# Binning: the spreading copies move from ScalarE to GpSimd, and four lane columns from VectorE to ScalarE

## The reference, cut to what matters

```
x = layernorm(x + L0(x, w, a, src, dst))       # exp(leaky_relu([x[src], x[dst]] @ w) @ a), normalised per src, summed per dst
x = layernorm(x + L1(x, W, A_left, A_right))   # four heads, normalised per src, summed per src
```

## Time and profile before

| | us |
|---|---|
| median of 3 runs | 3259.68 (3258.47 to 3259.81) |
| span of the profiled execution | 3274.5 |
| PE busy | 3060.7 (93%) |
| DVE busy | 3045.9 (93%) |
| ACT busy | 2750.1 (84%) |
| POOL busy | 155.0 (5%) |

### The profile page before, as it was taken

The page is one execution under the profiler, slowest core; times in us unless marked ns, Lnnn a source line. Parts: engine busy times, 40 slices in busy tenths (PEclk is TensorE's granted clock), DMA queues, the critical chain, the costliest instruction groups (busy, mean ns, idle before and its releaser), DMA issues. The chain is left out here.

```text
span 3274.5 us, 101508 instructions
## 1 busy us (share of the span) xinstructions
PE 3060.7 (93%) x40072; PEld 2792.8 (85%) x40072; DVE 3045.9 (93%) x4921; ACT 2750.1 (84%) x6946; POOL 155.0 (5%) x249
## 2 busy tenths in 40 slices
PE   5777699999999999699999999989999999999996
PEld 4666677778777877699999999988999999999994
DVE  8999889999999997799999999989999999999997
ACT  6988888888888885799999999987888888888887
POOL 0000000000000000000000000000111111111110
PEclk9989899999999997799999999999999999999998
DMA  3000022222222222234333333334455545554541
GB/s 66 13 14 11 23 98 93 87 93 94 93 87 93 94 86 48 65 96 97 97 97 96 97 96 97 97 93 137 161 163 160 164 161 163 161 163 161 162 151 41
DMA packets 173823, 333.06 MB, mean 102 GB/s; under 512 B 54876, under 2 KB 109616, under 8 KB 173264
## 3 DMA queue, kind: packets, MB, share of 16 engines
q1 hardware_dynamic: 170996, 323.30, 32.5%
q10 hardware_dynamic: 2348, 3.20, 0.4%
HBM read 320.77 MB, written 5.66 MB: 100 GB/s over the span
## 5 line engine op out<-in xcount | busy, mean ns | idle before, releaser
L1009 PE MATMUL l_gathered<-xp,l_src_onehot 128*128 128x128 bf16 x7203 | 467.0, 221 | 11.2 <-DVE l_src_onehot L922 11.2
L1436 PE MATMUL l_gathered<-hp,l_onehot 128*128 128x128 bf16 x7203 | 458.5, 219 | 0.0
L704 PE MATMUL sc_z<-sc_onehot,pq 128*128 128x256 f32 (+1 forms) x2450 | 429.4, 298 | 23.3 <-DVE sc_leaky L617 18.3
L1009 PEld LDWEIGHTS l_gathered<-xp,l_src_onehot 128*128 128x128 bf16 x7203 | 407.9, 99 | 26.3 <-DVE l_src_onehot L922 11.7
L788 ACT ACTIVATE sc_leaky<-sc_z 128x1024 f32<-128x1024 f32 (+3 forms) x325 | 309.8, 953 | 143.3 <-PE sc_z L708 140.5
L617 DVE SCALAR_TENSOR_TENSOR sc_leaky<-sc_z,sc_leaky 128x1024 f32<-128x1024 f32 (+3 forms) x325 | 370.1, 1139 | 60.0 <-ACT sc_leaky L788 52.5
L847 DVE TENSOR_TENSOR l_lane<-iota_b,l_lane_pairs 128x896 bf16<-128x896 bf16 x686 | 421.0, 614 | 0.0
L1436 PEld LDWEIGHTS l_gathered<-hp,l_onehot 128*128 128x128 bf16 x7203 | 406.1, 98 | 0.4
L708 PE MATMUL sc_z<-sc_onehot,pq 128*128 128x256 f32 (+1 forms) x2450 | 400.9, 286 | 0.0
L1450 PE MATMUL l_acc<-e,l_lane_wide 128*128 128x132 f32 x2744 | 385.5, 283 | 0.3 <-ACT e L1514 0.3
L704 PEld LDWEIGHTS sc_z<-sc_onehot,pq 128*128 128x128 f32 x2450 | 344.6, 196 | 35.9 <-issue 34.5
(11 more groups left out here) (246 smaller groups left out, 6107.4 us busy)
## 6 DMA issues: line engine op xcount, KB each, us to landing
rows_got<-edge_rows_wide SPq DMA_DIRECT2D x338, 448.0 KB, 3.7
l_got<-edge_rows_src SPq DMA_DIRECT2D x343, 224.0 KB, 3.2
placed<-edge_rows SPq DMA_DIRECT2D x144, 512.0 KB, 3.7
out_dram<-X SPq DMA_DIRECT2D x12, 256.0 KB
S<-edge_rows_wide SPq DMA_DIRECT2D x5, 448.0 KB, 8.4
edge_rows<-e SPq DMA_DIRECT2D x98, 6.1 KB
edge_rows_wide<-e SPq DMA_DIRECT2D x98, 12.2 KB
sc_last_rows<-edge_rows SPq DMA_DIRECT2D x24, 64.0 KB, 3.5
```

What stands on the lines that cost most here:

```text
L704: nc.tensor.matmul(z[:, b, 0:nw, :], PQ[:, b0 + b, q, 0:C], hot[:, r % HOTS, b, 0, 0:nw, :], start=(b == u and q == 0), stop=False)
L1009: ins = nc.tensor.matmul(gps[:, t % 2, i * P:(i + 1) * P], hot[:, t % RING, i, :], parts[:, g * GX + i, q, :], start=(q == 0), stop=(q == 2))
L1436: ins = nc.tensor.matmul(gps[:, t % 2, i * P:(i + 1) * P], dst_hot[:, t % RING, i, :], hp[:, g * GX + i, q, 0:C], start=(q == 0), stop=(q ...
```

## The change

`LATE` goes from 8 to 12, so `EARLY` from 28 to 24: DVE compares 24 lane columns and ACT makes 12. ACT's `spread_key` is gone. POOL gets a queue of its own in the binning, with the two copies of each window in the same buffers: the three column sets as one instruction of 128x756, then the key (128x648).

```
-    HALF, LATE = W_T // 2, 8
+    HALF, LATE = W_T // 2, 12
...
+            @block.gpsimd
+            def _(pool):
+                def spread(n):
+                    if n in (0, 1, FIRST, SECOND):
+                        pool.wait_ge(s["keyed"], 1 + (0, 1, FIRST, SECOND).index(n))
+                    elif n % CHUNK == 0:
+                        pool.wait_ge(s["keyed"], n // CHUNK + 4)
+                    if n >= SPREADS:
+                        pool.wait_ge(s["payload"], n - SPREADS + 1)
+                    nc.gpsimd.tensor_copy(wide[:, n % SPREADS], k.placed[:, :, n, :].unsqueeze(3).to_broadcast([P, 3, W_T, BLK_G])
+                                          ).then_inc(s["spread"], 1)
+
+                def spread_key(n):
+                    if n >= 1:
+                        pool.wait_ge(s["same"], n)
+                    nc.gpsimd.tensor_copy(key_b, k.key[:, n, :].unsqueeze(2).to_broadcast([P, W_T, HALF])).then_inc(s["key_spread"], 1)
+
+                for n in range(NB):
+                    spread(n)
+                    spread_key(n)
...
-                def spread_key(n):
...
-                    if n >= SPREADS:
-                        act.wait_ge(s["payload"], n - SPREADS + 1)
-                    for a in range(3):
-                        ins = nc.scalar.copy(wide[:, n % SPREADS, a], k.placed[:, a, n, :].unsqueeze(2).to_broadcast([P, W_T, BLK_G]))
-                    ins.then_inc(s["spread"], 1)
-                    if n >= 1:
-                        act.wait_ge(s["same"], n)
-                    nc.scalar.copy(key_b, k.key[:, n, :].unsqueeze(2).to_broadcast([P, W_T, HALF])).then_inc(s["key_spread"], 1)
-
...
-                spread_key(0)
-                spread_key(1)
...
-                    if 2 <= n + 3 < NB:
-                        spread_key(n + 3)
```

## The result

The changed kernel takes 3293.25 us (median of 4, 3293.1 to 3294.74) where the kernel before takes 3259.74 beside it: ratio 1.0106, 95% interval 1.0092 to 1.012, so +33.5 us. The likeliest case was forecast at 3306 and the range was 3244 to 3350.

A forecast was written before the change was run, and what follows sets the result against it. The prediction took DVE to bound the binning: +1.24 us a window standing for POOL's copies, -0.27 for fewer columns, +0.97 times 47 = +46 us. 3274.5 + 46 = 3320.5, less 14.8, gave 3305.7, predicted 3306, range 3244 to 3350.

The forecast's parts named there:

- The likeliest case: In the binning DVE stands for the copies at POOL's write rate: +0.97 us a window, 3306 us; chance 0.51.
- DVE is the bound of the binning: In the binning a window costs what DVE's chain costs, 7.27 us, with ACT busy 6.79.
- Four columns fewer, 0.27 us: DVE's lanes comparison drops 512 of 3584 elements, 0.27 us a window, all of it on the path.
- ACT 6.79 + 0.03 = 6.82 us: ACT's binning window gains 1.57 us and loses 1.54, staying under DVE's 7.00 us and costing nothing.
- POOL's copies and DVE's two-input instructions exclude each other: In the binning 6.94 of DVE's 7.27 us read two SBUF tiles; POOL can't copy without DVE standing or must wait.
- 1.24 us a window in which DVE stands: POOL's two copies in the binning take 1.40 us, of which the reduce hides 0.16.
- 47 windows: Binning windows by which the change of +0.97 us a window was multiplied, giving +46 us.
- No contention: Rival: copies run under DVE, whose reads lose under 0.27 us a window; window 7.00 us, 3247 us; chance 0.16.
- Starved: Rival: POOL gets no turn until DVE waits for its copies; +1.31 us a window, 3321 us; chance 0.14.
- Slow copies: Rival: POOL's copies take 3.4 us a window; +2.97 us a window, +140 us, 3399 us; chance 0.12.
- Evens out: Rival: copies at or below the low price (0.66 us), or ACT's longer chain eating the 0.27; 3260 us; chance 0.07.
- The rows of layer 1: Profile rows of POOL's L1390 and L1399 beside DVE, read as both sides losing time when they meet.

The follow-up runs named there:

- lanes_only: The kernel before with ScalarE comparing twelve lane columns and still making all copies, nothing on GpSimd: 3287.3 us, ratio 1.009.
- idle_copies: The kernel before with GpSimd making the same two copies into tiles nobody reads, ScalarE still making the used ones: 3304.8 us, ratio 1.0142.
- idle_writes: The kernel before with GpSimd writing constants of the same size into two unread tiles, reading nothing: 3259.0 us, ratio 1.0002.
- idle_half: The kernel before with GpSimd making half of each copy (128x378 and 128x324) into unread tiles: 3278.1 us against 3259.8, ratio 1.0067.
- waits_only: The kernel before with 49 more VectorE waits on a semaphore long reached, nothing else: 3255.9 us against 3258.9, ratio 0.9996.

## Why the prediction was right

- **DVE is the bound of the binning.** Held: the window grew by what DVE's instructions grew.
- **Four columns fewer, 0.27 us.** 0.27, by lanes_only.
- **ACT 6.79 + 0.03 = 6.82 us.** Held: it is busy 6.80 us in the window from 304.77 to 312.79. Its wait for the rank sum was forecast at 1.4 us a window and is 1.29 and 1.22 in the two windows around 305 and 313 us. ACT is never what DVE waits for in the plain window.
- **POOL's copies and DVE's two-input instructions exclude each other.** Held, shown by idle_copies against idle_writes.
- **1.24 us a window in which DVE stands.** The mis-sized term: it was 1.00 (0.48 + 0.52). The price of an element was right, 0.8 ns, and that was partly luck: it came from two instructions that read nothing (0.10 us between them), while idle_writes shows that what POOL only writes costs DVE nothing. It served because POOL's rate is much the same either way: (0.82 - 0.50)/378 = 0.85 ns an element for copies and (732 - 637)/108 = 0.88 ns for constants. The fixed 0.14 us of each instruction, taken from a POOL instruction of one element, was not: by idle_half DVE loses next to nothing that is fixed. Without it the sum is 1404 x 0.80 - 0.16 = 0.96. The cover by the reduce, put at 0.16, was 0.60 - 0.48 = 0.12. The 0.24 us too much, times 47, are 11 of the 12.5 us between +46 and +33.5.
- **47 windows.** The times are +0.75 x 47 = 35, with 34.5 measured at the end of the stage; here the count does no harm, because DVE bounds the windows with `place_keys` too. In lanes_only it did.
- **The rivals.** No contention: refuted, DVE's reads lose 1.00 us, not under 0.27. Starved: refuted; DVE waits for POOL's copies only three times, 2.4 us in all and before 90 us, and a waiting POOL gets its turn between two DVE instructions that follow without a gap (L244 and L259). Slow copies: refuted, 0.80 ns an element. Evens out: no; the low bound's 0.47 ns a read, from L1351's 0.12 us, was too low; why L1351 lost no more than that wasn't tried.
- **The rows of layer 1.** Two were read too broadly. POOL's L1399 in the earlier trace rows isn't alone: for 0.32 of its 0.57 us DVE's L1343 runs, which has one input from PSUM. And L1298, beside which L1399 takes 0.98 us, has one SBUF tensor as its input, not two, so that row shows another meeting than those of the binning.

## What to carry to other kernels

A spare GpSimd is no spare for a stage that VectorE bounds with instructions that have two SBUF inputs: every element it reads there is taken from VectorE's time, here 0.80 ns each, and the work taken off ScalarE has to be worth more than that. It was worth 0.27 us against 1.00. Under the reduce, which has one input, from PSUM, GpSimd's reads were free for 252 elements, and they pay where they fit in and are released early enough to stand ready; what GpSimd only wrote cost nothing. Whether a single input from SBUF leaves GpSimd alone too wasn't tried in the binning. Before moving work between two engines, see by how much the second is below the first, window by window and averaged with the windows that do extra work: here, without GpSimd, there was room for one column.

## What the runs showed of the hardware

- The loser waits for the instruction in progress to end, then the next is held: the key copy waited for the multiply L244 (1.53 us reported, 0.64 for the same elements only written), and the instruction that paid was the one behind it. The reported length of a POOL instruction is not what it costs DVE: 1.48 us on average for a loss of 0.52.
- An instruction of VectorE can begin 3.4 us sooner in a later stage through 49 waits that do nothing, as waits_only showed.
- In layer 1 DVE's L1343 multiplies a PSUM tile by an SBUF tile, and POOL's L1399 ends 0.49 us into it (2306.83 against 2306.34; 0.48 to 0.50 us in all 48 batches in which they meet). L1343 takes 0.94 us there and loses nothing against its median:

```profile
L1343 DVE TENSOR_TENSOR e<-l_gathered,l_weight x343: 939/949/959, 2238.1 to 3217.5; 128x768 f32<-128x768 f32 x172
```

- One SBUF input isn't always harmless to POOL: L1399 starts under L1298, a `tensor_scalar` of one bf16 SBUF tensor, in 48 of its 49 instances and each time ends 0.40 to 0.42 us behind L1298's end, whether it started 0.30 us ahead of that end or 0.57, as if it did its work only then. L1298 itself takes at most 0.69 us.
- TensorE's granted clock can fall while TensorE is at work: in the profiled execution of before it went from 1.00 (2.4 GHz) to 0.50 (1.2 GHz) at about 1263 us, with PE busy 11.33 of the 12 us up to 1262, and the stage of edge scores took 899 us where it took 880 or 881 in the thirteen other profiles. In waits_only and idle_writes the same part of the stage ran at 1.00, and the clock fell only after the last start of L704's line there. Why it fell early in the one stays open.
